# ScalarE fetches rows beside SyncE, VectorE makes all copies, gram products follow the next unit's transposes

## The reference

```python
x = relu(dense @ W0 + b0)            # 13 -> 512
x = relu(x @ W1 + b1)                # -> 256
dense_out = relu(x @ W2 + b2)        # -> 64
emb = tables[f][sparse[:, f]]        # 26 tables of 12500 rows of 64
gram = einsum('bid,bjd->bij', emb, emb)
interact = gram[:, TRIU_I, TRIU_J]   # 325 pairs of each sample
y = concatenate([dense_out, interact], 1) @ Wt + bt   # -> 256
```

## Time and profile before

| | us |
|---|---|
| median of 3 runs (lowest, highest) | 537.41 (536.21, 539.76) |
| the profiled execution, device time | 535.61 |
| its span, first to last instruction | 533.8 |
| PE busy in the span | 345.1 (65%) |
| DVE busy | 206.8 (39%) |
| ACT busy | 203.7 (38%) |
| POOL busy | 389.7 (73%) |
| mean granted clock of TensorE, share of full speed | 0.760 |

### The profile page before, as it was taken

How to read it: one execution, slowest core, us unless ns; L and a number is a source line. 1 busy time by engine, 2 the same in 40 slices (tenths; PEclk the granted TensorE clock), 3 DMA queues, 4 the chain that set the end, 5 groups by cost and what they waited for, 6 DMA issues and landing times.

```text
span 533.8 us, 8006 instructions
## 1 busy us (share of the span) xinstructions
PE 345.1 (65%) x1744; PEld 285.4 (53%) x1744; DVE 206.8 (39%) x648; ACT 203.7 (38%) x637; POOL 389.7 (73%) x414
## 2 busy tenths in 40 slices
PE   2067854895846965658747786369854487617975
PEld 1055743674635854537636665257643376516864
DVE  6432344334324343244443342432451425314353
ACT  2023444345224453144432452433541436313462
POOL 6777777777777777777777777777777777777760
PEclk9555887769767788677877697685895869757699
DMA  5214112221122212221212211222212221122110
GB/s 101 46 28 91 27 28 32 33 38 28 27 38 38 28 27 29 38 37 28 29 26 38 39 27 30 38 28 37 28 28 37 38 30 26 28 38 35 27 26 21
DMA packets 23182, 18.66 MB, mean 35 GB/s; under 512 B 12775, under 2 KB 16585, under 8 KB 23116
## 3 DMA queue, kind: packets, MB, share of 16 engines
q0 software_dynamic: 13024, 13.36, 17.8%
q1 hardware_dynamic: 6612, 2.52, 2.2%
q10 hardware_dynamic: 3498, 2.26, 1.4%
HBM read 15.20 MB, written 2.10 MB: 32 GB/s over the span
## 4 chain that ended last, share of the span: by engine, by line
POOL 72%; issue 23%; PE 1%; DVE 1%; DMA 1%; POOLq 0%
POOL emb L283 72%; PE mlp_ps L573 1%; DVE gram L198 1%; DMA emb<-in_L_rec_tables_dram,row_idx 1%; DMA raw_idx<-n_r_sparse_features_dram 0%; PE gram_ps L560 0%; POOLq L79 0%; PE rowsT_ps L543 0%; POOLq L278 0%; DVE out_sb L372 0%; DVE embT L184 0%; DVE wrap L313 0%; DVE row_idx L323 0%; DVE wrapped L317 0%; DVE capped L314 0%
## 5 line engine op out<-in xcount | busy, mean ns | idle before, releaser
L283 POOL DMA_INDIRECT emb<-in_L_rec_tables_dram,row_idx x407 | 388.9, 956 | 127.5 <-issue 123.8
L198 ACT COPY gram<-gram_ps 32x48 f32<-32x48 f32 (+1 forms) x512 | 122.9, 240 | 151.0 <-PE gram_ps L560 145.2
L198 DVE COPY gram<-gram_ps 32x48 f32<-32x48 f32 (+1 forms) x512 | 122.2, 239 | 124.6 <-PE gram_ps L560 117.7
L560 PEld LDWEIGHTS gram_ps<-embT 128*128 128x128 f32 x1024 | 144.5, 229 | 17.2 <-issue 9.4
L560 PE MATMUL gram_ps<-embT 128*128 128x100 f32 x1024 | 148.5, 312 | 4.1 <-DVE embT L184 4.1
L543 PE MATMUL rowsT_ps<-ident,emb 128*128 128x128 f32 (+1 forms) x215 | 49.5, 341 | 157.0 <-DMA emb<-in_L_rec_tables_dram,row_idx 135.6
L184 DVE COPY embT<-rowsT_ps 64x512 f32<-64x512 f32 (+2 forms) x96 | 65.0, 689 | 154.2 <-PE rowsT_ps L543 153.8
L543 PEld LDWEIGHTS rowsT_ps<-ident,emb 128*128 128x128 f32 (+1 forms) x215 | 28.1, 163 | 175.5 <-DMA emb<-in_L_rec_tables_dram,row_idx 129.8
L184 ACT COPY embT<-rowsT_ps 64x512 f32<-64x512 f32 x64 | 53.4, 861 | 109.1 <-PE rowsT_ps L543 108.6
L573 PE MATMUL mlp_ps<-w_gram,gram 128*128 128x256 f32 x224 | 72.3, 485 | 1.9 <-DVE gram L198 1.9
L573 PEld LDWEIGHTS mlp_ps<-w_gram,gram 128*128 128x128 f32 x224 | 57.3, 260 | 14.3 <-DVE gram L198 2.3
(11 more groups left out here) (28 smaller groups left out, 39.8 us busy)
## 6 DMA issues: line engine op xcount, KB each, us to landing
by_hand<-in_L_rec_tables_dram SPq DMA_DIRECT2D x1152, 0.2 KB
emb<-in_L_rec_tables_dram,row_idx POOLq DMA_INDIRECT x407, 2.7
out_dram<-out_sb ACTq DMA_DIRECT2D x16, 128.0 KB, 1.9
w_gram<-w_tri SPq DMA_DIRECT2D x3, 192.0 KB
w_sb<-in_L_rec_W_dram SPq DMA_DIRECT2D x1, 512.0 KB
raw_idx<-n_r_sparse_features_dram SPq DMA_DIRECT2D x2, 182.0 KB, 3.9
w_gram<-w_tri SPq DMA_DIRECT2D x1, 224.0 KB
x_sb<-in_r_dense_features_dram ACTq DMA_DIRECT2D x1, 104.0 KB, 2.8
```

The costliest lines, as they stand in the source:

```text
L198: last = copy(gram[FP * g:FP * (g + 1), q, t0:NS, c0 + a0 * SQ + s:c0 + a1 * SQ:SQ], gram_ps[FP * s:FP * (s + 1), a0:a1, src:src + SQ * (N ...
L283: nc.gpsimd.indirect_dma_start(emb[:, j, k, :], None, tables_v[:, :], bass.IndirectOffsetOnAxis(ap=row_idx[:, r * UR + j, k:k + 1], axis=0 ...
L560: last = nc.tensor.matmul(gram_ps[:, a, 0:SQ * (F - 1)], samples.rearrange("p s f -> p (s f)"), samples[:, :, 1:F], start=True, stop=True)
```

## The change

- `BY_HAND` grows from 9 to 17 units. SyncE fetches the last pair's rows for units 4, 7, 10, 14, 17, 20, 23, 27, 30, ScalarE for units 5, 8, 11, 15, 18, 22, 25, 29. `fetch_rows` is now shared by both. ScalarE's fetches come in 32 pieces of 32 rows, and its stores of results stand between them.
- VectorE makes all copies out of the transposes, all relus and all gram copies. The gram copies of a unit are no longer split in halves: 16 instructions with both halves' columns. Only for the last two units (`TAIL` and `LAST_UNIT`) do both engines copy, half by half as before.
- TensorE's order: the products of unit n stand behind the transposes of unit n+1. They wait for `gram_ready`, all gram copies of unit n-1.
- The third chunk's transpose goes to the first PSUM bank, behind the copies of the first chunk.

```diff
-    BANK = [0, 1, 1]
-    BY_HAND = [4, 7, 10, 13, 16, 19, 22, 25, 28]
+    BANK = [0, 1, 0]
+    SP_UNITS = [4, 7, 10, 14, 17, 20, 23, 27, 30]
+    ACT_UNITS = [5, 8, 11, 15, 18, 22, 25, 29]
+    BY_HAND = SP_UNITS + ACT_UNITS
...
+                    if n != LAST_UNIT and len(CHUNKS[c]) > 1:
+                        rowsT_evac(nc.vector.tensor_copy, c, 1, j).then_inc(embT_odd[c], 1)
...
-                for half in range(2):
-                    dve.wait_ge(gram_in_psum, (r * UR + j) * 2 + half + 1)
-                    gram_evac(nc.vector.tensor_copy, DVE_BLOCKS, j, half).then_inc(gram_evac_dve, 1)
+                dve.wait_ge(gram_in_psum, (r * UR + j) * 2 + 2)
+                gram_evac(nc.vector.tensor_copy, BLOCKS, j, 0, NG).then_inc(gram_ready, 1)
...
+            def relu(out, in_, bias):
+                return nc.vector.tensor_scalar(out, in_, bias, 0.0, ALU.add, ALU.max)
...
+            def vector_round(r):
+                embT_evac(r, 0)
+                if r > 0:
+                    gram_blocks(r - 1, 3)
+                embT_evac(r, 1)
+                if r > 0:
+                    out_evac(r - 1, 1)
+                gram_blocks(r, 0)
+                l0_evac(r)
+                embT_evac(r, 2)
+                gram_blocks(r, 1)
+                l1_evac(r)
+                if r < ROUNDS - 1:
+                    embT_evac(r, 3)
+                    l2_evac(r)
+                    gram_blocks(r, 2)
+                    out_evac(r, 0)
+                else:
+                    l2_evac(r)
+                    dve.wait_ge(top_in_psum[1], r)
+                    gram_blocks_tail(TAIL)
+                    out_evac(r, 0)
+                    embT_evac(r, 3)
+                    gram_blocks_tail(LAST_UNIT)
...
+            pieces = [(n, c0) for n in ACT_UNITS for c0 in range(0, P, LOADED)]
+            stores = [(4 * r + 3 + 2 * q, r, q) for r in range(ROUNDS) for q in range(2)]
+            act.wait_ge(hand_idx_ready, 1)
+            for i, (n, c0) in enumerate(pieces):
+                for ready, r, q in stores:
+                    if ready * 7 // 6 + 2 == i:
+                        store(r, q)
+                fetch_rows(act, n, c0, c0 + LOADED)
...
+                    if c == LAST:
+                        pe.wait_ge(embT_even[0], n + 1)
+                        pe.wait_ge(embT_odd[0], n + 1)
+                    else:
+                        wait_if_any(pe, embT_even[c], n)
+                        wait_if_any(pe, embT_odd[c], n)
+                        if c == 0:
+                            wait_if_any(pe, embT_even[LAST], n)
...
                 pe.wait_ge(embT_even[LAST], n + 1)
                 pe.wait_ge(embT_odd[LAST - 1], n + 1)
+                wait_if_any(pe, gram_ready, min(n, TAIL))
...
+            def tensor_round(r):
                 transposes(r, 0)
+                if r > 0:
+                    gram_products(r - 1, 3)
+                transposes(r, 1)
+                if r > 0:
+                    top(r - 1, 1)
                 gram_products(r, 0)
                 mlp_l0(r)
+                transposes(r, 2)
                 gram_products(r, 1)
                 mlp_l1(r)
+                if r < ROUNDS - 1:
+                    transposes(r, 3)
                 mlp_l2(r)
                 gram_products(r, 2)
+                top(r, 0)
+                if r == ROUNDS - 1:
+                    transposes(r, 3)
+                    gram_products(r, 3)
```

More of the change, by code:

```diff
@@ L180, in rowsT_evac @@
             ks = CHUNKS[c]
-            i = (ks.start - 8 * BANK[c]) // 2
             m = len(ks[odd::2])
@@ L201, in gram_evac, with fetch_rows @@
             return last
+        def fetch_rows(eng, n, first, stop):
+            i, at = BY_HAND.index(n), n % 2 * NP + n // 2
+            for c0 in range(first, stop, LOADED):
+                _, offs = nc.values_load_multi_w_load_instructions(
+                    hand_off[at:at + 1, c0:c0 + LOADED], engines=[eng.engine], min_val=0,
+                    max_val=(F * VOCAB - 1) * ROW,
+                    skip_runtime_bounds_check_because="DVE has clamped the rows to their tables")
+                for c, off in enumerate(offs, c0):
+                    row = c % 2 * US + c // 2
+                    eng.dma_start(by_hand[row:row + 1, i, :].bitcast(mybir.dt.uint8),
+                                  tables_bytes[bass.ds(off, ROW)].rearrange("(a e) -> a e", a=1)
+                                  ).then_inc(by_hand_in[i], 16)
         def wait_if_any(eng, semaphore, count):
@@ new lines, in _ @@
+            for ready, r, q in stores[:-2]:
+                if ready * 7 // 6 + 2 >= len(pieces):
+                    store(r, q)
+            act.wait_ge(top_in_psum[1], ROUNDS - 1)
+            for half in range(2):
+                act.wait_ge(gram_in_psum, TAIL * 2 + half + 1)
+                gram_evac(nc.scalar.copy, ACT_BLOCKS, TAIL % UR, half * HG, (half + 1) * HG).then_inc(gram_tail_act, 1)
+            act.wait_ge(gram_in_psum, (LAST_UNIT - 1) * 2)
+            for c in range(LAST):
+                act.wait_ge(rowsT_in_psum[c], NU)
+                rowsT_evac(nc.scalar.copy, c, 1, UR - 1).then_inc(embT_odd[c], 1)
@@ L606, in _ @@
+            for r in range(ROUNDS):
                 tensor_round(r)
```

174 lines of the change are left out of this document (53 added, 121 removed).

## The result

The changed kernel takes 563.2 us (median of 4 runs, 560.6 to 564.6) against 537.5 before: ratio 1.047, 95% interval 1.044 to 1.050. It is slower, as forecast, but by 26 us instead of 12, and 3 us above the range's upper end.

What follows compares the result with a forecast made beforehand. TensorE and VectorE waiting in turn were to bound the kernel: third products of round 0 end at 84.4, seven rounds of 63.8 less 2.4, a 19.1 us tail, 547.7 us of span, forecast 549; range 531 to 560.

Steps and rivals of the forecast that it cites:

- the circuit: TensorE and VectorE waiting for each other in turn: 63.8 us a round against 62.3 of gathers, so it becomes the bound.
- Cost zero, hidden behind GpSimd: ScalarE's row fetches: 50.7 us a unit, 406 us for eight, never late, so no cost.
- 4 gram copies: VectorE's joined gram copies for a round's four units: 5.5 us each, 22.0 us a round.
- 4 first pairs: VectorE's even and odd copies of a unit's first eight row pairs, in sequence: 2.14 us each, 8.6 a round.
- 4 gram products: TensorE's products: three a round start at the lower clock, 5.9 us each, the fourth takes 3.8; together 21.5 us.
- last transposes, top layer, third layer: Once-a-round steps on TensorE: last transposes 1.3 us, odd half's top layer 5.4, dense layer before the third products 1.3.
- Rival B: Faster: cheap gram copies on VectorE let the products run at 3.8 us; 532.1 us, chance 0.15.
- the 4.7 us floor: Lowest price of a unit's gram copies on VectorE, from the output copy's 0.84 ns an element: 274 and 298 ns.
- rival C: ScalarE's new row stream stretches gathers or brings unit 29 late; a 1.28 us gather adds 12 us; chance 0.03 with D.
- A: Gathers stay the bound and their gain is given back in the tail: no change, 537.3 us, chance 0.30.
- D: TensorE's products all at 7.0 us and VectorE's gram copies at 5.7: 71.1 us a round, 600; chance 0.03 with rival C.
- The signs: Expected in the trace: gram copies near 325 and 358 ns, fewer row waits, GpSimd waiting for transposes, rounds of 63 to 65 us.

Runs made afterwards that it cites:

- experiment 1: The changed kernel without ScalarE's row stream (nine units, SyncE's, 407 gathers): 557.98 us, ratio 1.038 to the kernel before.
- experiment 4: The changed kernel without ScalarE's row stream, ScalarE again copying the odd row pairs and 8 of 16 joined gram blocks: 542.91 us, ratio 1.011.
- experiments 5 and 6: 5: changed kernel plus unread matmuls on TensorE, behind its wait 580.83 us, ahead of it 559.19 us; 6: the latter without ScalarE's row stream, 552.97 us.
- experiment 10: The changed kernel, ScalarE fetching only the first 64 of 256 bytes of each of its rows: 563.33 us, ratio 1.049.

## Why the prediction was right in kind and too low

The case and its mechanism came as forecast: slower, by the circuit. The step that took the time out of the range is "Cost zero, hidden behind GpSimd", for ScalarE's row stream: it costs 5 us, and without it the median is 558.0 (experiment 1), inside 531 to 560. The second is a term of the circuit, transposes, top layer, third dense layer and handovers: 8.8 us predicted, 10.2 measured.

The predicted span was 547.7, the measured one 558.8, and the median stands 4.4 us above that span where I had added 1.8. The 1.8 held for the profiled execution (560.6), but it is the fastest of four; the others took 562.6, 563.9 and 564.6, with mean granted clocks of 0.747, 0.705 and 0.706 against its 0.762. The 11.1 us of span are 4.2 at the start, 5.8 in seven rounds and 1.1 in the tail. Term by term, for the round from 280.6 to 345.5 us, 64.9 against the predicted 63.8:

| term | predicted | measured |
|---|---|---|
| 4 gram copies | 22.0 | 5.51 + 5.48 + 5.49 + 5.52 = 22.0 |
| 4 first pairs | 8.6 | 2.04 + 2.07 + 2.04 + 2.04 = 8.2 |
| 4 gram products | 21.5 | 6.59 + 3.71 + 6.61 + 4.82 = 21.7 |
| relus, output copy | 2.9 | 2.4 + 0.4 = 2.8 |
| last transposes, top layer, third layer (the prediction's "second dense layer"), handovers | 8.8 | 10.2 |

- **Gram copies.** Right. The strided rows of before gave 322 to 333 and 353 to 368 ns for forms that the trace did not have; measured 324 and 354. Rival B fell with this term, and so did the 4.7 us floor. The Trainium skill's price (VectorE: DVE Perf Modes, TRN2 errata) gives an estimate of 3.9 us a unit; the 5.5 us disagree again.
- **Row copies.** 1009 ns where one engine reads the bank, 1070 where ScalarE reads beside it, 1054 in experiment 4, where it does so again: 0.4 us better a round.
- **Relus.** I took 0.41 us from VectorE's copy of the same shape; they are 478 ns, above both rows that I had as bounds (408 and 470). Back to back four take 1.66 us, 0.41 each, since they overlap, and the term comes out right by luck.
- **The step that failed in the round** is the last line of the table, +1.4 us. The handover from VectorE's pair to the last transpose took 0.25 to 0.41 us, not 0.06: I had read the handovers off the quiet end of the run. The odd top layer with its dense product stands 5.9 us in the circuit, at the lower clock, for 5.4 as the mean of all 16; the third layer's products take 1.97 us for a mean of 1.3. The means of before mix both clocks, and in the new order these steps stand behind waits.
- **Products.** The mean forecast (5.4) was right (5.45), by errors that cancel: of the three that stand behind a wait, forecast at 5.9 each, two take 6.6 and one 4.8; experiments 5 and 6 show that the clock is worth about 5 us of the whole, where nothing else holds.
- **The start.** I took unit 3's rows at 76.9 as in the earlier trace rows; its last transpose is at 80.86, since the gathers land late from the first unit on. Without the stream it is at 76.92, the third products end at 83.5, and 84.4 was forecast.
- **ScalarE's stream at no cost.** Wrong, and the main reason for leaving the range. SyncE kept its pace (21.3 to 479.0), GpSimd its 1.25 us a gather. ScalarE ran from 17.1 to 469.5, 56.6 us a unit instead of 50.7: some 54 a unit by itself, and three units of 59 to 67, in which it stood at a store (the first until 94.7 us). Its last unit was ready near 470, not 430, still ahead of the 480 at which it was wanted. A quarter slower would not have been just in time, as I wrote: 20 + 1.25 x 406 is 527; 13% is what there was room for. I had looked at issue times alone, and rival C was priced only for slower issue. The landing was the column to watch.
- **Rivals.** A's bound is what experiments 4 and 6 show when the circuit is taken down, and its longer tail shows in 4 (24.1 us behind the last gather for 16.7); both have 407 gathers, so that the gathers' gain would go into this tail is not shown. C came another way: neither longer gathers nor a late unit 29, but late landings. D did not occur.
- **The signs.** The forms of the gram copies, the waits and GpSimd's share of the chain came as listed. "GpSimd with waits for the transposes late in the run" did not: it waited for none.
- **The range.** Its top came from a circuit of 65.4 with everything else fixed. The circuit was 64.9; the start and the median's distance from the profiled execution, together 6.8 us, had no width of their own.

## What to carry to other kernels

When work is gathered on one engine, count what two engines wait for in turn, unit by unit, from the rows; that sum was good to 2%, while busy shares (58% for VectorE) said nothing. Price steps that will stand behind a wait at the clock of rows that stand behind a wait, never at a mean over both. A stream of tiny transfers that costs nothing at its issuer may cost much at the receiver of someone else's, 5 us here: read the time to landing of every other transfer, and how many of them the median is made of, and thin the stream before giving it up.

## What the chip showed that was not expected

A second stream of 256-byte rows delays gathers that have nothing to do with it. One stream of 2.5 rows a us leaves a gather at 2.7 us; two take it to 9.1 (14.6 to 18.2 from 320 to 460 us; 15 gathers resolved), and output stores from 1.9 to 10.7. The two queues in experiment 1, without the second stream:

```profile
q1 hardware_dynamic: 6612, 2.52, 2.2%
q10 hardware_dynamic: 3498, 2.26, 1.3%
```

ScalarE's 1024 rows add 2048 packets to its queue (5546 less 3498), two for a row, and 0.27 MB; yet the packets of the two queues together take 9.7% of 16 engines' time instead of 3.5. That is 6.2% of 16 x 558.8 us, 554 us; 270 ns for each added packet. SyncE's queue, with no packet more, went from 2.2 to 5.1%. These times are not all work. Row packets of the two queues overlap in the trace: from 120 to 460 us those of 256 bytes and less add up to 438 us, and one of them is under way in 245 of the 340. So they hold waiting too, and that 554 us is near one engine's span says nothing of how busy an engine is: with a quarter of the bytes (experiment 10) the same sum, 7.1% less 3.5, is 323 us, and the delay is the same.

One reading is an engine that both streams share, where a part of every gather and store queues behind the rows: each row is one data packet and one semaphore packet, each gather 32 packets (12768 for 399), and a gather has landed only when the last of its parts has. The profile does not name the engines, so it stays an inference. The Trainium skill, DMA: Bandwidth & Descriptors, in the section on why a DMA increments its semaphore by 16, says that a transfer issued by SyncE or ScalarE uses the lowest-numbered of the engines, as many as it is split over. By that rule transfers of one data packet from both would meet on the same engine; no run here shows it.
